# Moving expert-gate arithmetic, weight splits and four row gathers inside a two-layer mixture-of-experts kernel

## The reference, cut to what matters

```
xf = layernorm(x)                       # 4096 x 256
probs = softmax(xf @ Wg)                # 8 experts
top_vals, top_idx = top_k(probs, 2)
loc  = place of each choice in its expert's list, in order (first choices of all tokens, then second)
keep = loc < C                          # C = 1280
gates = top_vals * keep
gates = gates / maximum(gates.sum(-1), 1e-9)
out_e = (gelu(inp @ W_in[:, :512]) * (inp @ W_in[:, 512:])) @ W_out    # per expert, 1280 slots
y = sum over the 2 choices of gates * out_e at the choice's slot
x = x + 0.5 * y
```

## Time and profile before

| what | value |
|---|---|
| median of 3 runs | 1628.39 us (1625.16 to 1634.05) |
| the profiled execution | 1625.16 us |
| its span in the trace | 1623.3 us |
| PE busy | 1441.1 us (89%) |
| DVE busy | 1025.8 us (63%) |
| ACT busy | 712.4 us (44%) |
| POOL busy | 683.8 us (42%) |
| mean granted TensorE clock | 0.941 of full speed |

### The profile page before, as it was taken

One profiled execution on the slowest core, in us unless ns is written; L12 is line 12 of the kernel. 1 busy time (PEld: TensorE's weight loads), 2 busy tenths in 40 slices (PEclk: granted clock), 3 DMA queues, 4 the chain that ended last, 5 costly groups with the idle time before them and its releaser, 6 DMA issues. The chain is left out here.

```text
span 1623.3 us, 25464 instructions
## 1 busy us (share of the span) xinstructions
PE 1441.1 (89%) x8838; PEld 1083.7 (67%) x8840; DVE 1025.8 (63%) x2607; ACT 712.4 (44%) x1116; POOL 683.8 (42%) x653
## 2 busy tenths in 40 slices
PE   4599999999645799999999999999876999999994
PEld 3589888889534455555555555555556899888884
DVE  7656665655275777777777778886376555665551
ACT  5333333333223055656566566666463333333331
POOL 1445566563423433333333332224305555556533
PEclk9699999999867699999999999999987999999997
DMA  9544444453377936666666578552174454444426
GB/s 310 167 81 99 98 87 78 98 105 34 45 215 217 253 113 164 174 164 164 164 163 177 146 181 260 161 169 93 42 246 110 82 96 98 97 99 68 95 30 136
DMA packets 125560, 218.27 MB, mean 134 GB/s; under 512 B 20232, under 2 KB 86280, under 8 KB 122312
## 3 DMA queue, kind: packets, MB, share of 16 engines
q1 hardware_dynamic: 88824, 165.56, 35.2%
q0 software_dynamic: 30720, 42.62, 16.8%
q10 hardware_dynamic: 5904, 8.66, 1.8%
HBM read 130.56 MB, written 90.14 MB: 136 GB/s over the span
## 5 line engine op out<-in xcount | busy, mean ns | idle before, releaser
L2023 ACT ACTIVATE a_wts<-a_s_psum 128x1024 f32<-128x1024 f32 (+1 forms) x384 | 300.9, 809 | 180.7 <-PE a_s_psum L2140 178.5
L923 POOL DMA_INDIRECT sums<-e_res,e_sum_row x160 | 254.1, 1588 | 286.3 <-ACT e_res L1062 260.7
L1899 DVE CUSTOM_DVE_ANT_0 a_m_psum<-a_m_psum,mask 128x128 f32<-128x128 f32 (+3 forms) x512 | 249.1, 502 | 127.5 <-PE a_m_psum L2115 119.5
L2115 PE MATMUL a_m_psum<-a_kp,a_qp 96*128 96x512 f32 (+2 forms) x768 | 287.9, 409 | 25.7 <-DVE a_parts L1899 10.2
L2115 PEld LDWEIGHTS a_m_psum<-a_kp,a_qp 96*128 96x128 f32 x768 | 148.0, 195 | 144.8 <-DVE a_parts L1899 61.5
L1050 ACT ACTIVATE e_act_a<-e_a_psum 128x512 f32<-128x512 f32 (+1 forms) x192 | 101.3, 528 | 273.2 <-PE e_a_psum L1128 273.2
L1847 POOL TENSOR_SCALAR_AFFINE_SELECT a_wts<-a_wts 128x512 f32<-128x512 f32 x128 | 78.2, 634 | 330.9 <-ACT a_wts L2023 330.9
L2140 PE MATMUL a_s_psum<-a_qp,a_kp 97*128 97x512 f32 (+2 forms) x768 | 209.7, 355 | 0.4
L968 DVE TENSOR_TENSOR e_hid<-e_act_a,e_g_psum 128x512 f32<-128x512 f32 (+1 forms) x192 | 114.7, 597 | 143.4 <-PE e_g_psum L1128 142.4
L253 POOL DMA_INDIRECT e_slots<-normalized,e_token x160 | 165.7, 1036 | 70.9 <-issue 47.5
L1147 PE MATMUL e_o_psum<-e_w_hi,e_h_hi 128*128 128x256 f32 x640 | 182.9, 286 | 0.0
(11 more groups left out here) (270 smaller groups left out, 2553.3 us busy)
## 6 DMA issues: line engine op xcount, KB each, us to landing
packs<-x_res SPq DMA_DIRECT2D x48, 512.0 KB, 5.8
e_w_raw<-in_W_in SPq DMA_DIRECT2D x16, 1024.0 KB, 8.3
a_qp<-packs SPq DMA_DIRECT2D x16, 1024.0 KB, 7.8
a_kp<-packs SPq DMA_DIRECT2D x16, 1024.0 KB, 13.7
e_w_raw<-in_W_out SPq DMA_DIRECT2D x16, 512.0 KB, 8.3
normalized<-r_xn SPq DMA_DIRECT2D x16, 512.0 KB, 4.3
sums<-x_res SPq DMA_DIRECT2D x2, 4096.0 KB, 16.5
x_res<-sums SPq DMA_DIRECT2D x8, 1024.0 KB, 11.2
```

What stands on the lines that cost most here:

```text
L923: nc.gpsimd.indirect_dma_start(sum_dram, bass.IndirectOffsetOnAxis(ap=sum_row[:, at:at + 1], axis=0), res[j][:], None, bounds_check=last_r ...
L1899: nc.vector.tensor_tensor_reduce(products, products, c["mask"][:, QC - width:], 1.0, MASKED, ALU.add, ALU.max, top).then_inc(max_read, 1)
L2023: nc.scalar.activation(wts[(u * NS + s) % 2][:, j, 0:w], s_ps[q % 2][:, 0:w], ACT.Exp).then_inc(weighed, 1)
L2115: nc.tensor.matmul(m_ps[bank((n, h, z))][:, 0:stream], qp[n % NB][0:PACK, h, qt * P:(qt + 1) * P], kp[n % NB][0:PACK, h, part * QC:part * ...
```

## The change

Six edits, all in `route` and `experts`, and so each made for both mixtures:

1. `EARLY_TILES = 6` becomes `FIRST_TILES = 2`: POOL issues two gathers of expert 0 at the end of `route` and eight at the start of `experts`.
2. The division by the sum of the kept gates is done once for all tokens in `route`. POOL gets three more instructions (`kept`, and two for `sums`), DVE a reciprocal of 128x32 behind the second piece of `is_within`, and only then does POOL form `gates`.
3. POOL's multiplication of `rk` no longer runs ahead; it stands behind the wait for `slot`.
4. `gates()` in `experts` shrinks from seven DVE instructions to three.
5. ACT's three `weights_high` stand together behind the exponentials, and DVE's two `weights_rest` stand behind `rows_and_choices` of the first ten columns.
6. For r = 1, group 7 is normalized by ACT, between `turned(3)` and `taken(1)`, and no longer by DVE.

```diff
-EARLY_TILES = 6
+FIRST_TILES = FIRST_CHUNKS[0][1] // P
...
-        BY_ACT = (1, 2, 3) if r == 0 else (0, 1, 2, 3, 4, 5)
+        BY_ACT = (1, 2, 3) if r == 0 else (0, 1, 2, 3, 4, 5, 7)
...
-                pool.wait_ge(numbered, 2)
-                pool.wait_ge(hot_ready, CH * TOPK)
+                pool.wait_ge(slots_summed, 1)
                 link(nc.gpsimd.tensor_scalar(keep[:], rk[:], float(CAP), None, ALU.mult))
-                pool.wait_ge(slots_summed, 1)
                 link(nc.gpsimd.tensor_tensor(keep[:], keep[:], slot[:], ALU.add))
                 nc.gpsimd.tensor_scalar(keep[:], keep[:], float((EXP + 1) * CAP), None, ALU.is_lt).then_inc(kept_ready, 1)
                 pool.wait_ge(kept_ready, 1)
                 pool.wait_ge(weighed, CH)
+                link(nc.gpsimd.tensor_tensor(kept[:], best[:], keep[:], ALU.mult))
+                link(nc.gpsimd.tensor_tensor(sums[:], kept[:, 0, :], kept[:, 1, :], ALU.add))
+                nc.gpsimd.tensor_scalar(sums[:], sums[:], 1e-9, 2.0, ALU.max, ALU.mult).then_inc(kept_ready, 1)
+                pool.wait_ge(kept_ready, 3)
                 for k in range(TOPK):
-                    nc.gpsimd.tensor_tensor(gates[:, :, k], best[:, k, :], keep[:, k, :], ALU.mult).then_inc(gates_ready, 1)
+                    nc.gpsimd.tensor_tensor(gates[:, :, k], kept[:, k, :], sums[:], ALU.mult).then_inc(gates_ready, 1)
...
-                for j in range(EARLY_TILES):
+                for j in range(FIRST_TILES):
                     gather_slots(nc.gpsimd, held, xn_dram, 0, j)
...
                 choose(0)
                 centre(0)
-                for z in range(FIRST_PARTS):
-                    weights_rest(z)
                 choose(1)
...
+                    if z == 1:
+                        dve.wait_ge(kept_ready, 2)
+                        nc.vector.reciprocal(sums[:], sums[:]).then_inc(kept_ready, 1)
...
                 rows_and_choices(slice(0, ST), 1)
+                for z in range(FIRST_PARTS):
+                    weights_rest(z)
                 dve.wait_ge(piece_read, 2 * PIECES)
...
                     taken(0)
                     turned(2)
                     turned(3)
+                    act.wait_ge(deviated, 3)
+                    normalize(7)
                     taken(1)
...
-                weights_high(0)
                 taken(2)
                 turned(6)
                 turned(7)
-                weights_high(1)
                 taken(3)
                 exponentials(0)
                 exponentials(1)
-                weights_high(2)
+                for z in range(len(W_PARTS)):
+                    weights_high(z)
...
-                for j in range(EARLY_TILES, ST):
+                for j in range(FIRST_TILES, ST):
                     gather_slots(nc.gpsimd, held, xn_dram, 0, j)
...
-                        nc.vector.tensor_tensor(both[:], of[:, :, D], of[:, :, D + 1], ALU.add).then_inc(gate_parts, 1)
                         for k in range(TOPK):
-                            nc.vector.tensor_tensor(by_choice[k][:], of[:, :, D + k],
+                            nc.vector.tensor_tensor(by_choice[k][:], slots[u][:].rearrange("p (j w) -> p j w", w=ROW)[:, :, D + k],
                                                     held["choice"][k][:, bass.ds(e * ST, ST)], ALU.mult).then_inc(gate_parts, 1)
-                        dve.wait_ge(gate_parts, parts + 1)
-                        nc.vector.tensor_scalar(both[:], both[:], 1e-9, 2.0, ALU.max, ALU.mult).then_inc(gate_parts, 1)
-                        dve.wait_ge(gate_parts, parts + 4)
-                        nc.vector.tensor_tensor(by_choice[0][:], by_choice[0][:], by_choice[1][:], ALU.add).then_inc(gate_parts, 1)
-                        nc.vector.reciprocal(both[:], both[:]).then_inc(gate_parts, 1)
-                        dve.wait_ge(gate_parts, parts + GATE_PARTS)
+                        dve.wait_ge(gate_parts, (e + 1) * TOPK)
                         dve.wait_ge(res_ready, (e + 1) * ST)
-                        nc.vector.tensor_tensor(gate[u][:], by_choice[0][:], both[:], ALU.mult).then_inc(gate_ready, 1)
+                        nc.vector.tensor_tensor(gate[u][:], by_choice[0][:], by_choice[1][:], ALU.add).then_inc(gate_ready, 1)
```

## The result

The changed kernel took 1643.58 us (median of 9 executions, 1637.51 to 1647.89) against 1629.56 us for the kernel before (median of 9): ratio 1.0081, interval 1.006 to 1.01. The medians lie 14.0 us apart, and the ratio makes 13.2 us: slower, and clear of the noise. The same kernel profiled again later, at its median, gives the sum further down.

What follows compares the result with a forecast made beforehand. TensorE was taken to bound `experts`, a chain over ACT, PE and DVE `route`. Seams 2.2 + 2.5, gathers 3.9 + 3.7 and clock 2.3 make 14.6 us on 1625.16, 1643 us after the median's 3.2 us offset; range 1633 to 1649.

Steps and rivals of the forecast that it cites:

- Gathers of tiles 2 to 5: Opening of `experts`: PE waits for tiles gathered behind the seam, landing behind expert 1's weights; 3.9 and 3.7 us.
- The clock: Opening of `experts`: the wait makes TensorE run at half clock again; 2.3 us, counted for one of two mixtures.
- both starts repeated: Opening of `experts`: whole waits and a slow clock restart in both mixtures; 16.9 to 18 us, 1645 to 1646; no separate chance.
- The seam: Between `route` and `experts`: DVE closes the block, next start 2.7 us behind it; +2.2 and +2.5 us.
- The lower bound of 2.3: Between `route` and `experts`: least distance in us from DVE's end to the next start, three quarters of POOL's.
- the new seam hides: Between `route` and `experts`: distance behind DVE much shorter than POOL's, seams about 2.9 us together, 1641; 0.20 shared with clock holding.
- POOL's distance was not what I took it for: Between `route` and `experts`: the conclusion to draw if the seam moves less than 1.3 us.
- The division: In `route`: later `gates` and transfer, first gathers after 58.1 us; hidden by more than 4 us with two gathers.
- Splits, `keep`, reciprocal: DVE's chain in `route`: splits add 1.4 us, `rk` behind `slot` 0.5, reciprocal 0.4; DVE's end moves 2.3 us.
- Group 7: Second mixture's `route`: four normalizations on ACT make `choose(1)` 0.95 us later; DVE gains nothing.
- `gates()`: In `experts`: fewer DVE instructions save some 10 us of DVE time, none on PE's path; nothing, at most 2.9 us a stage.
- its upper terms: Highest values of the seams, gather waits (4.3 each) and clock restarts (2.9 twice), behind the range's top of 1649 us.

Runs made afterwards that it cites:

- after_third: The changed kernel, unchanged, run and profiled again on another chip: 1643.17 us, ratio 1.0084 to the kernel before.
- two_gathers: The kernel before with two early gathers in place of six, nothing else: 1654.16 us, ratio 1.0068 to the kernel before.
- before_four: The kernel before with four early gathers in place of six: 1624.68 us, ratio 0.9977 to the kernel before.
- gates_in_route2: The kernel before with edits 2 to 4 of the change alone (gates normalized in `route`): 1635.68 us, ratio 1.004.
- after_six: The changed kernel with six gathers in `route` again in place of two: 1649.0 us, ratio 1.0046 to the kernel before.
- after_pause_late: The changed kernel with POOL's expert 1 gathers held until expert 0's chunks are transposed, and expert 1's weights loaded after tiles 2 to 5 landed: 1633.49 us, ratio 1.0025.
- before_again2: The kernel before, unchanged, run again for its records on the second chip: 1629.48 us, ratio 1.0001.
- after_again: The changed kernel, unchanged, run again for a second profile on the first chip of the experiments: 1659.01 us, ratio 1.0096 to the kernel before.
- first group: Four runs on one chip: the changed kernel again, two early gathers, six early gathers, late weights; 1649.0 to 1659.01 us, the kernel before 1642.65 there.
- The pause: The changed kernel with POOL waiting for all three transposed chunks of expert 0 before expert 1's ten gathers: 1641.87 us, ratio 1.0073 to the kernel before.
- splits_moved2: The kernel before with edit 5 of the change alone (weight splits moved): 1630.33 us, ratio 1.0005.

## Why the prediction was right or wrong

**The total, 1643 us, was right; the largest term was right in its mechanism, and the seams were not. That the sum still met the measured time is in part luck:** the first seam was put about 2 us too high and the waits together 1.4, the clock 2.2 too low, and some 3 us of the measured time have no place yet. By the prediction's steps:

- *Gathers of tiles 2 to 5*: predicted waits of 3.9 and 3.7 us (the second is 3.6 by its own numbers, 1248.1 less 1244.46); measured 3.5 and 3.2, and 2.7 and 3.5 in `after_third`, where the fourth gather landed after 5.9 and 6.1 us and not 6.7. The mechanism was right and shown: hold back the weights and the wait is 0.2 or none.
- *The clock*: predicted 2.3 us for one mixture. Both paid, 2.0 and 2.5 us in `after_third`, as in the rival "both starts repeated", with smaller waits beside it. The Trainium skill's page ("TensorE: Matmul & The Clock Gate", The HAM clock gate) says that the low clock is the default and that activity releases it; by it both restarts are paid, and the trace agrees: both mixtures of `after_third` read 0.50 behind the wait, for 3.4 and 5.8 us.
- *The seam*: this is the step that failed, "If DVE closes it instead, the distance is at most 2.82; I take 2.7". The distance behind DVE is 1.0 to 1.1 us (after 1.0, `two_gathers` 1.1, `before_four` 1.0). DVE's end was forecast at 66.7 and came at 66.1, so PE started at 67.1, moved by 0.0 to 0.4 us in place of 2.2. The lower bound of 2.3 had been set at three quarters of POOL's distance for no row at all; the earlier trace rows showed DVE's end only where POOL closed the block, and bound its distance from above alone. The rival "the new seam hides" described this; its 2.9 us were not worked out, and with 1.0 us behind DVE's predicted ends of 66.7 and 1236.7 they would have been 1.8. The sign named for a seam that moves less than 1.3 us, "POOL's distance was not what I took it for", points at the wrong term: POOL's distance held, at 2.9 to 3.1 us, wherever POOL closed the block.
- *The division*: "hidden, by more than 4 us. Had POOL still six gathers, this would be paid" was right on both counts: paid in `gates_in_route2` with 3.3 us at the seam, hidden here. Its own times were late: two gate products on POOL took 2.29 us where the earlier trace rows had led me to 0.4 each, and the first gather went out at 59.3, not 58.1.
- *Splits, `keep`, reciprocal*: DVE's end moved by 1.7 us in place of 2.3; from the end of `slot` it is 1.9 (20.5 us against 18.5). Alone, the gates cost 0.9 and the splits 1.4 on this count, both as forecast. The reciprocal took 0.34 (forecast 0.3, with its gap 0.4). `choose` gained nothing by the removal: DVE waits 3.4 us for PE there instead.
- *Group 7*: its 0.95 us was not measured alone. `after_six`, which is the gates, the splits and group 7 without the moved gathers, is at 1.0046, and the first two alone at 1.004 and 1.0005. In the traces the copy behind it starts 3.8 us after that of `turned(2)` in place of 3.1: 0.7 us. `choose(1)` then begins 38.2 to 43.5 us into the second `route` in the eight records with group 7 on ACT (mean 40.8), and 37.6 to 41.4 us in the six without it (mean 38.8). That is the forecast direction, but the spread within each set is larger than the difference.
- *`gates()`*: nothing, as forecast (338.6 against 338.5 us).

The sum by the profile at the median: waits 6.2 and clock 4.5 us, together 10.7, and 9.6 by the ratios. The rest of the 13.7 us (1.0084) is 3 to 4 us, which `after_pause_late` has left (1.0025, interval 1.8 to 6.4 us). Where it lies is open, and one pair of records can't show it. `after_third` is 12.4 us longer than `before_again2`: 0.4 to the first seam, 4.7 and 6.0 to the first results, 0.4 in the two bodies of `experts`, less 1.0 in the second `route`, and 2.0 between the mixtures, where nothing was edited. But these last two differ as much between records of the kernel before itself: its second `route` took 66.5 and 70.1 us to PE's start, and the stretch between the mixtures 739.6 and 743.7 us. The second `route`, with group 7 in it, is a place where the rest may lie.

Seen as edits: gates in the route +6.5 us, splits +0.8, and the exchange of four gathers from before to behind the seam about +6 (1.0046 to 1.0084, on different chips) or +8 (to 1.0096, on one chip). By the records that exchange is 10.7 for waits and clock, less the seams that it gives back: from the end of `slot` to PE's start it is 25.0 us in `after_six` and 21.8 in `after_again`, so 3.2 us for each mixture and 4.3 in all. The two countings don't close by some 2 to 4 us, the same open rest.

One bound of the prediction is loose: its upper terms (5.3 for the seams, waits of 4.3 twice, 2.9 twice) give 1648 and not 1649.

**What causes the "remote" stalls is not settled.** They were in the first record of the change and in all four of the first group's chip, where the kernel before also took 13 us more than elsewhere. They were in none of the nine other records, one of them the changed kernel unchanged. At nine of the ten places the last of the stalled engines went on 2.8 to 4.0 us after POOL had issued the last gather of expert 1, at the tenth (the first mixture of `two_gathers`) 0.9 us before it. The pause, made to test this, met a chip on which they did not occur.

What they cost can be read. In the first record it is 38.8 and 35.0 us from PE's start to the first results, in `after_third` 29.7 and 31.0: 13.1 of the 13.3 us by which the spans differ. So they made that one execution long, and not the median. `after_six` has no gather wait and 34.0 and 28.1 us there against 25.0, 12 us of stalls, in an execution at its own median. Yet it is only 7.5 us over the kernel before on its chip, and its edits alone explain that much (6.5 and 0.8). So the kernel before must have lost about as much on that chip, which fits its 13 us; no record of it there was taken, so this is inferred. They carry little of the 0.8%: the ratio is 1.0084 where the record has none, and 1.0096 where it has.

## What to carry to other kernels

Where a block ends for all engines, find for each engine its own distance from its last instruction to the next block, in a record where that engine is the last; a distance read where another closes the block is an upper bound and nothing more. Work taken out of one side of such a seam is paid on the other if it is needed early there: count how long after the seam its result is used, and what big transfer starts at the seam with it. And when one wait is traced to a transfer, try the number between (four gathers, not six or two) before giving up the idea.

## What the runs showed of the hardware that was not expected

- A block that POOL closes with a gather is left 2.9 to 3.1 us after the gather's end (to POOL's next start, five kernels); one that DVE closes, 1.0 to 1.2 us after DVE's (to PE's start, six kernels). Why they differ was not tried.
- Elementwise products of 128x32 on POOL took 1.1 us each (2.29 for two, 2.29 and 2.30 in other records) beside DVE's bf16 operations of 128x2048; the sum of 128x32 some 4 us earlier, with no such operation beside it, took 0.25 in `after_third`. That DVE's work is the cause was not tried by itself. For a gather it was: the one issued at 61.7 us took 0.95 us in `before_again2` and 1.77 in `splits_moved2`, where DVE's two 128x1024 subtractions had been moved beside it.
- In the first mixture of `after_third` the granted clock read 0.50 up to a wait of 2.7 us, 1.00 for the first 1.2 us behind it, and fell to 0.50 only then, for some 3 us. In the second, and in the first record of the change, it was 0.50 at once. A wait's price in clock can thus stand well behind the wait, and a look at the first matmuls alone would miss it.
